# Spherical numbers of the fourth and fifth chunk copied over the rows by DMA from memory instead of by selector products

## What is computed

```python
acc = sh[:, 0:1] * (x_e @ C[:, 0, :])
for s in range(1, S):                      # S = 9, C is [64, 9, 128], once for keys and once for values
    acc = acc + sh[:, s:s + 1] * (x_e @ C[:, s, :])
return acc * w
...
attn = jnp.einsum('ehd,ehd->eh', q[edge_src], k)
upd = jax.ops.segment_sum(v * alpha[..., None], edge_src, num_segments=n)   # alpha: softmax per node and head
```

## Time and profile before

| | |
|---|---|
| three runs | 2995.71, 3005.49, 3006.69 us (median 3005.49) |
| the profiled execution | 3001.06 us, span 2999.2 us, mean granted TensorE clock 0.899 |
| busy share of the span | PE 84%, DVE 88%, ACT 51%, POOL 59% |
| DMA | 415.29 MB, mean 138 GB/s |
| loop over groups | from about 458 us to the end of the 196 groups at about 2900 us |

### The profile page before, as it was taken

The page is one execution under the profiler, slowest core; times in us unless marked ns, Lnnn a source line. Parts: engine busy times, 40 slices in busy tenths (PEclk is TensorE's granted clock), DMA queues, the critical chain, the costliest instruction groups (busy, mean ns, idle before and its releaser), DMA issues.

```text
span 2999.2 us, 48368 instructions
## 1 busy us (share of the span) xinstructions
PE 2506.8 (84%) x12505; PEld 1789.6 (60%) x12505; DVE 2631.2 (88%) x3781; ACT 1531.1 (51%) x2914; POOL 1778.8 (59%) x1719
## 2 busy tenths in 40 slices
PE   2233357999999999999999999999999999999714
PEld 1232325667776766777667776777667776776511
DVE  6688736899999998999999999999899999999737
ACT  1321234556656665566566565566566666666310
POOL 2700027777777776777677776777677777776030
PEclk7555557999999999999999999999999999999855
DMA  6786713344444444444444444444444444444340
GB/s 183 208 228 183 195 40 91 87 127 148 143 142 145 143 139 136 141 144 140 136 138 141 146 141 137 141 143 142 136 138 141 145 141 138 147 144 128 108 135 11
DMA packets 282404, 415.29 MB, mean 138 GB/s; under 512 B 64463, under 2 KB 191875, under 8 KB 278470
## 3 DMA queue, kind: packets, MB, share of 16 engines
q1 hardware_dynamic: 222278, 296.67, 31.5%
q0 software_dynamic: 52704, 107.19, 13.9%
q10 hardware_dynamic: 7128, 8.13, 0.8%
HBM read 309.59 MB, written 102.20 MB: 137 GB/s over the span
## 4 chain that ended last, share of the span: by engine, by line
PE 55%; DVE 21%; issue 9%; DMA 6%; ACT 4%; SPq 2%; POOL 1%; DVEq 1%; POOLq 0%; ACTq 0%
PE bank L1117 12%; PE bank L1119 10%; PE bank L1118 10%; PE bank L1162 5%; PE bank L1141 5%; DVE run_c L1429 4%; DVE xa_t L1537 4%; DMA keep_c<-keep_d 3%; DVE z_l L1545 3%; ACT z_h L875 2%; PE bank L1124 2%; PE bank L1123 2%; PE bank L1193 2%; DVE val L1574 2%; PE bank L1112 2%
## 5 line engine op out<-in xcount | busy, mean ns | idle before, releaser
L744 POOL DMA_INDIRECT gathered<-xtab_d,src_g x784 | 831.9, 1061 | 448.8 <-PE bank L1094 191.8
L744 POOL DMA_INDIRECT gathered<-qtab_d,dst_g x784 | 810.0, 1033 | 256.0 <-issue 250.7
L1117 PE MATMUL bank<-z_h,wt_h 128*128 128x512 f32 x1568 | 745.5, 475 | 51.8 <-DVE val L1574 49.1
L875 ACT ACTIVATE z_h<-xa_t 128x512 fp32r<-128x512 f32 x980 | 620.5, 633 | 289.1 <-DVE xa_t L1537 176.5
L1537 DVE TENSOR_TENSOR xa_t<-bank,r_r 128x512 f32<-128x512 f32 x980 | 662.8, 682 | 3.7 <-PE bank L1141 1.2
L1119 PE MATMUL bank<-z_h,wt_l 128*128 128x512 f32 x1568 | 621.0, 396 | 0.0
L1118 PE MATMUL bank<-z_l,wt_h 128*128 128x512 f32 x1568 | 620.2, 396 | 0.0
L1545 DVE TENSOR_TENSOR z_l<-xa_t,z_h 128x512 fp32r<-128x512 f32 x784 | 536.1, 684 | 85.8 <-ACT z_h L875 70.1
L1117 PEld LDWEIGHTS bank<-z_h,wt_h 128*128 128x128 f32 x1568 | 302.0, 193 | 112.7 <-issue 71.9
L1141 PE MATMUL bank<-s,sel 128*128 128x512 bf16 x980 | 349.5, 389 | 2.6 <-DVE xa_t L1537 2.1
L1119 PEld LDWEIGHTS bank<-z_h,wt_l 128*128 128x128 f32 x1568 | 295.0, 188 | 71.6
(11 more groups left out here) (222 smaller groups left out, 3952.8 us busy)
## 6 DMA issues: line engine op xcount, KB each, us to landing
nrow_d<-x_r SPq DMA_DIRECT2D x196, 288.0 KB
ea<-in_ea_t SPq DMA_DIRECT2D x392, 128.0 KB
exb<-exd_d SPq DMA_DIRECT2D x392, 128.0 KB
dmb<-exd_d SPq DMA_DIRECT2D x392, 128.0 KB
ea_c<-in_ea_t SPq DMA_DIRECT2D x49, 512.0 KB, 5.0
aggrow_d<-xa_t SPq DMA_DIRECT2D x49, 512.0 KB, 3.8
gathered<-xtab_d,src_g POOLq DMA_INDIRECT x784
gathered<-qtab_d,dst_g POOLq DMA_INDIRECT x784
```

The source lines that it names most:

```text
L744: rows_in = pool.indirect_dma_start(rows[:, c % 4, k, :], None, table, bass.IndirectOffsetOnAxis(ap=picked[:, s, at:at + 1], axis=0))
L875: act.activation(z_h[:, c % 2, i, :], z[:, i, :], ACT.Copy).then_inc(zh_ok, 1)
L1117: pe.matmul(ps[:, :], wt_h[rows, w, :], high, start=start, stop=False)
```

## The change

For chunks 3 and 4 the spread numbers come from memory. SP gets `load_harmonics`, at the end of its body(c) for group c+3: one load that copies numbers 6 and 7 to 64 rows each (`sh_3`), one that copies number 8 to 128 rows (`sh_4`). Both add to `ea_in`, the semaphore on which `edge_high` waits, so its count per group goes from 32 to 64. The loads are issued when all five chunks of group c+1 have been made (z_ok). PE spreads NS = 3 chunks instead of 5. DVE's `outer` for chunks 3 and 4 reads SBUF instead of PSUM.

```diff
+        sh_3 = x_flat[:, 2 * G + 8 * RW:4 * G + 8 * RW].rearrange("p (b g) -> p b g", b=2)
+        sh_4 = [r_r[:, :, :].rearrange("p t d -> p (t d)")[:, 2 * G:3 * G], xa_t[:, NJ * G:(NJ + 1) * G]]
...
+            def load_harmonics(j, c):
+                past(sp, z_ok, j, c, 2, NJ)
+                hold()
+                sp.dma_start(sh_3[:, c % 2, :], harmonics_t[6:8, bass.ds(group(j, c) * G, G)]
+                             .rearrange("s (o w) -> s o w", o=1).to_broadcast([2, D, G])).then_inc(ea_in[c % 2], 16)
+                sp.dma_start(sh_4[c % 2], harmonics_t[8:9, bass.ds(group(j, c) * G, G)].to_broadcast([P, G])
+                             ).then_inc(ea_in[c % 2], 16)
...
+                if live(j, c + 3):
+                    if isinstance(j, int) and c == -3:
+                        sp.wait_ge(qtab_out, 16)
+                    load_harmonics(j, c + 3)
...
-                landed(act, ea_in, j, c, 32)
+                landed(act, ea_in, j, c, 64)
...
-                if not isinstance(j, int) or c * NJ + i >= 2:
+                if i >= 2:
                     done(pe, z_ok, j, c, NJ, i - 1 - NJ)
-                pe.matmul(bank[2 + (NJ * c + i) % 2][:, :], sel[:, i, :], s3[:, c % 4, :], start=True, stop=True
+                elif not isinstance(j, int) or c >= 1:
+                    done(pe, z_ok, j, c - 1, NJ, i + 2 - NJ)
+                pe.matmul(bank[2 + (NS * c + i) % 2][:, :], sel[:, i, :], s3[:, c % 4, :], start=True, stop=True
...
-                    if i + 2 < NJ and live(j, c + 1):
+                    if i + 2 < NS and live(j, c + 1):
                         spread(j, c + 1, i + 2)
...
-                done(dve, shb_ps, j, c, NJ, i + 1 - NJ)
-                dve.tensor_tensor(z[:, i, :], bank[2 + (NJ * c + i) % 2][:, :], xt[:, c % 2, :], ALU.mult
-                                  ).then_inc(z_ok, 1)
+                if i < NS:
+                    done(dve, shb_ps, j, c, NS, i + 1 - NS)
+                    spread_sh = bank[2 + (NS * c + i) % 2][:, :]
+                else:
+                    landed(dve, ea_in, j, c, 64)
+                    spread_sh = sh_3[:, c % 2, :] if i == NS else sh_4[c % 2]
+                dve.tensor_tensor(z[:, i, :], spread_sh, xt[:, c % 2, :], ALU.mult).then_inc(z_ok, 1)
```

More of the change, by code:

```diff
@@ L29 @@
 NW = 2 * NJ + 2
+NS = 3
 H = 8
@@ L506, in arrived, with loads_and_stores @@
                 eng.wait_ge(ring[b], (g - b + n) * (per // n))
-        def loads_and_stores(sp, edges_t):
+        def loads_and_stores(sp, edges_t, harmonics_t):
             sp.dma_start(x_r[:, :, 0:D], a["x"].rearrange("(t p) d -> p t d", p=P)).then_inc(x_in, 16)
@@ L584, in load_edge @@
                                  ).then_inc(ea_in[c % 2], 16)
-                past(sp, shb_ps, j, c, 4, NJ)
+                past(sp, shb_ps, j, c, 4, NS)
                 hold()
@@ L678, in _ @@
                 sp.dma_start(shf[:, :], sh_s.rearrange("s (c w) -> (s c) w", c=SC)).then_inc(sh_in, 16)
-                loads_and_stores(sp, ea_s)
+                loads_and_stores(sp, ea_s, sh_s)
             with sp.Else():
                 sp.dma_start(shf[:, :], a["sh_t"].rearrange("s (c w) -> (s c) w", c=SC)).then_inc(sh_in, 16)
-                loads_and_stores(sp, a["ea_t"])
+                loads_and_stores(sp, a["ea_t"], a["sh_t"])
             sp.wait_ge(out_ok, 1)
```

## The result

| | before | changed |
|---|---|---|
| median (lowest to highest) | 3003.86 us (2995.71 to 3006.69), 4 runs | 3234.68 us (3228.07 to 3240.91), 4 runs |
| ratio, 95% interval | | 1.0772 [1.0745, 1.0800] |
| profiled execution | 3001.06 us, clock 0.899 | 3231.47 us, span 3229.6, clock 0.883 |

The change makes the kernel 7.7% slower, 231 us. The page of the changed kernel (outer is L1559 now, its products L1132 to L1134, edge_high L873, the scan L1632, the spread L1158, the loads of sh_3 and sh_4 L599 and L601): span and counts, packets, the two queues, the chain that ended last by engine and by line.

What follows compares the result with a forecast made beforehand. It took the two DMA engines carrying sh_3 as the changed kernel's bound: 190 bodies x (13.8 - 12.0) = 342 us on 3001.06 gives 3343, plus 4 for the median, so 3350 us; range 3100 to 3520.

Steps and rivals of the forecast that it cites:

- Who bounds the kernel before: Loop bodies: DVE alone sets 11.35 us; PE decides only in plain bodies of 11.43 us, by 0.08 us.
- The spreads, 13 us: PE, two spreads fewer a body: 0.48 us gained in seven bodies, 28 times, 13 us.
- DVE's operands in SBUF, nothing: DVE's two products reading SBUF instead of PSUM: 681 against 682 ns, so the move costs nothing.
- Loads on 16 engines land in time: New loads before ACT's edge_high: about 10.9 us available, 5.0 us median landing, so 16 engines would hide the wait.
- The load of sh_3 goes through two engines: The sh_3 load, [2, 64, 512]: its outermost dimension confines 128 rows of 2 KB to two engines, 64 each.
- 13.8 us a body: On sh_3's two engines: 7.06 us existing work, 0.79 for sh_4, 6.1 for sh_3; 13.95, taken as 13.8, for 190 bodies.
- The exponents' store: SP, one body in seven: issued behind the new loads, it would hold SP several us; not added to the sum.
- All alike: Sign in the changed profile: bodies of about 13.8 us, all alike, with the batch's hardly longer.
- SP's issues at 0.4 to 0.6 us: SP's two new load issues a body: 0.4 to 0.6 us each, filling a gap in its queue.
- The wide spreading at 2990 us: Rival: sh_3 uses 16 engines or the two keep up; only the spreads' gain counts, 2990 us; chance 0.10.
- Late, but not full: Rival: the two engines have gaps but loads land late; 12.6 us a body, 3115 us; chance 0.10.
- PE's clock: Rival: idle PE is granted the lower clock, 1.2 GHz, for stretches; 3600 us and more; chance 0.08.

Runs made afterwards that it cites:

- the two halves: Changed kernel with the sh_3 load split into two loads of [64, 512], one number to 64 rows each, same bytes: 2990.56 us, ratio 0.9967 to the kernel before.
- The unread load: Kernel before, all five spreads kept, plus one [2, 64, 512] load a body whose data nobody reads: 3083.75 us, ratio 1.0275.
- the kernel with the store first: Changed kernel with SP issuing the exponents' store ahead of the new loads instead of behind them: 3167.37 us, ratio 1.0552 to the kernel before.
- both loads on two engines: Changed kernel with the sh_4 load also written as [2, 64, 512], numbers 7 and 8: 4108.88 us, ratio 1.3694 to the kernel before.
- the turned dimensions: Changed kernel with sh_3 still one load but its 64 copies outermost, [64, 2, 512]: 2992.93 us, ratio 0.9964 to the kernel before.
- four engines: Changed kernel with the sh_3 load written as [4, 32, 512], numbers 4 to 7 to 32 rows each: 3005.36 us, ratio 1.0012 to the kernel before.
- with exb and dmb on 16 engines and the store first: Changed kernel with exb and dmb loaded copies outermost, [16, 8, 256], and the exponents' store ahead of the new loads: 3024.84 us, ratio 1.0092 to the kernel before.

## Why the prediction was right, and where its numbers were off

- **Who bounds the kernel before**: borne out. With the two PE products gone and the loads spread, a plain body takes 11.35 us, what the body did in which PE had a gap.
- **The spreads, 13 us**: 13.05 between the medians, 11 to 19 by the interval of the ratio, so the mechanism is right and the match to a tenth is chance. The body with the turns fell from 13.28 to 13.01 us, by the 0.24 expected. The sign of 588 spreads shows in their weight loads (L1158: 588, three a group; before 980); of the products themselves the trace has only 393 records.
- **DVE's operands in SBUF, nothing**: borne out. From 600 to 2700 us:

```profile
L1559 DVE TENSOR_TENSOR xa_t<-bank,r_r 128x512 f32<-128x512 f32 x474 | 323.4, 682 | 0.0
L1559 DVE TENSOR_TENSOR xa_t<-x_r,r_r 128x512 f32<-128x512 f32 x158 | 108.4, 686 | 0.0
```

  The Trainium skill's 120 against 58 cycles ("VectorE: DVE Perf Modes", TRN2 errata) doesn't show in these durations.
- **Loads on 16 engines land in time**: borne out by the two halves, which leave no wait for them.
- **The load of sh_3 goes through two engines**: borne out. Small packets rose by 67,992 - 64,463 = 3,529, and 196 x 18 is 3,528. The unread load, which comes alone, gives 64,855 - 64,463 = 392, 2 a group. Written for 4 and 16 engines, the load of sh_3 gave just 2 and 14 more a group. The Trainium skill states this rule ("DMA: Bandwidth & Descriptors", "Use all 16 engines"); the trace agrees for 2, 4, 8, 9, 14 and 16.
- **13.8 us a body**: mis-sized. The failing term is the 6.1 us for sh_3, taken from the 47.8 ns per KB of a stretch with only exb, rows of 1 KB. A row of 2 KB costs 82 ns, so sh_3 takes 64 x 0.082 = 5.2 us and sh_4 0.65. 7.06 + 5.2 + 0.65 = 12.9 us, and 12.96 is what the kernel with the store first takes. So the 7.06 us, read from busy time, seem to add up in full; no run measures them by themselves. 12.3 us for the unread load against 12.5 measured is near, but no second check, since SP's stops are in the 12.5. The 190 bodies were too many: by them 0.96 us a body makes 182 us, and 167 are measured. In the changed kernel DVE's first scan starts at 624.13 us, before at 622.16, so the bodies ahead of it, most of which load no exponents yet, lost only 2 us.
- **The exponents' store**: named, its mechanism right, and left out of the sum, where it was held against the part of the 7.06 us that might not add up. It is worth 3234.68 - 3167.37 = 67 us. The two misses point opposite ways: 0.8 us a body too much on the engines, 0.35 too little on SP. With the bodies counted too high, that is why 3350 lay 115 us off and no more. The 3234.68 us lie 5 us inside the range 3230 to 3500 that was given to this mechanism, and only by the stop that the sum left out: without it the kernel takes 3167 us. That part is luck.
- **"All alike"** was wrong for that reason: SP's stop falls on one body in seven, and makes it 14.5 to 17.7 us.
- **SP's issues at 0.4 to 0.6 us**: right for sh_3, wrong for sh_4. From 600 to 2700 us, the issues of sh_4 into one of its two buffers (ns, lowest, median, highest) in the changed kernel, with the two halves, and with both loads on two engines:

```profile
L601 SPq DMA_DIRECT2D xa_t<-in_sh_t x79: 336/1247/3542, 606.3 to 2683.3; - x79
```

```profile
L603 SPq DMA_DIRECT2D xa_t<-in_sh_t x88: 435/445/590, 600.2 to 2685.2; - x88
```

```profile
L601 SPq DMA_DIRECT2D xa_t<-in_sh_t x59: 526/2838/3558, 615.3 to 2681.4; - x59
```

- **The rivals.** The wide spreading at 2990 us is what the two halves and the turned dimensions made: 2990.56 and 2992.93. *Late, but not full* is nearer than it looks. From 600 to 2700 us, where ACT waited, edge_high ran 13.3 us after the issue of its sh_3 load, and the issue two groups on came 12.3 us later (medians): 12.8 us a body, near what was measured. But such a sum must come out whenever ACT waits, whether the engines are full or not. Against this rival stand that with the store first at most one packet is under way for 0.1% of the time (though four engines, where 15 us are lost, also leave only 2.2%), and the unread load: nobody waits for it, and 87 us are lost. PE's clock stayed at 0.97 in the stretch, and PE was busy for 527 of 600 us, so it was not the bound; with both loads on two engines it was granted 0.85 with PE idle for a quarter of the time, and there too the engines set the pace.

What stays open: with exb and dmb on 16 engines and the store first, the sum gives 12.96 - 3.15 / 2 = 11.4 us a body, less than the 12.0 that DVE sets in the mean with two halves; so nothing should be lost. Its 346 issues of ea give 12.14, and 3025 us against the 2990 of the two halves. ACT waits 55 us in 2100 for the new loads, more than these 35 us, so the waits can account for all of them. Either the loads are late without full engines, the rival above, or the sum of 11.4 is too low: at most one packet is under way for only 0.4% of the time there. No run separates these two.

## What to carry to other kernels

Before a broadcast load is put into a loop, read its outermost dimension, and add up what the busiest engine gets from all queues in one body: copies outermost, or one load for each row, cost nothing measurable here where [2, 64, 512] cost 244 us. Small packets, counted in a profile, tell how many engines each form of transfer uses. A mean DMA share of 0.55, or 0.39, does not say that DMA has room; the slices in which only two engines' share is busy do say something. And a transfer whose data nobody waits for can still cost, 87 us here, through the stores and the issues behind it.

## What was not expected of the hardware

- **The issue itself is held.** When the two engines were full, SP stood inside its DMA instructions, with no wait for a semaphore: 1.25 us (median) for sh_4 where 0.45 is usual, 2.84 with both loads on two engines, and 6.69 and 3.94 us for pairs of ea loads that took 1.16 before. In the trace that is busy time of SP's queue (54% of the chain), not a wait. That a limit on outstanding work causes it is argued from when it appears, not shown.
- **Rows of 2 KB are a little cheaper per byte than rows of 1 KB** on one engine: 82 ns (81 in the stretch with two engines busy) against twice the estimate of 47.8 ns, where both are copies of one row in memory.
- **With half the rows on each engine, a sixteenth of the loss is left**: 32 rows on each of four engines lost 15 us against 16 engines, 64 on each of two 244.
